# The drain of a two-layer attention kernel: last unit transposed on TensorE, a new order, a split form for four tiles

## The reference, cut to what matters

```python
h = _layernorm(x) * (1 + ca) + sa
x = x + ga * _L1_attn_ref(h, ...)       # latent attention, 32 heads, softmax over 512 keys
h = _layernorm(x) * (1 + cb) + sb
x = x + gb * _L1_ffn_ref(h, W, lora_A, lora_B, magnitude)

# _L1_attn_ref, per head:  attn = softmax(query @ key.T * scaling);  out = attn @ v;  return out @ w_o
# _L1_ffn_ref:
eff_W = W + lora_B @ lora_A
column_norm = sqrt(sum(eff_W * eff_W, axis=1))
result = (x @ W.T + x @ lora_A.T @ lora_B.T) / column_norm * magnitude
```

## Time and profile before

| | us |
|---|---|
| median of 3 runs (lowest, highest) | 905.48 (903.23, 910.38) |
| profiled execution, its own time | 904.65 |
| span of its profile | 902.4 |
| busy: TensorE, VectorE, GpSimd, ScalarE | 820.7, 681.8, 538.9, 536.5 |

### The profile page before, as it was taken

The page is one execution under the profiler, slowest core; times in us unless marked ns, Lnnn a source line. Parts: engine busy times, 40 slices in busy tenths (PEclk is TensorE's granted clock), DMA queues, the critical chain, the costliest instruction groups (busy, mean ns, idle before and its releaser), DMA issues.

```text
span 902.4 us, 15065 instructions
## 1 busy us (share of the span) xinstructions
PE 820.7 (91%) x4560; PEld 540.4 (60%) x4560; DVE 681.8 (76%) x1322; ACT 536.5 (59%) x1158; POOL 538.9 (60%) x481
## 2 busy tenths in 40 slices
PE   3899993699996996899999999999999999999997
PEld 1588873578784874465656565665655656564543
DVE  4768896644453467998989898889898899897662
ACT  5668874624233785666666666665666666665522
POOL 3334432012122236998889888887888989897213
PEclk8899997799998898999999999999999999999899
DMA  8530000845235441666666666665566766665511
GB/s 330 216 119 2 1 2 9 227 117 176 89 105 151 123 130 38 168 153 152 153 154 155 154 153 155 153 156 143 131 156 185 184 154 155 149 156 138 125 35 70
DMA packets 91460, 120.07 MB, mean 133 GB/s; under 512 B 30387, under 2 KB 41651, under 8 KB 91381
## 3 DMA queue, kind: packets, MB, share of 16 engines
q1 hardware_dynamic: 66804, 85.54, 34.3%
q10 hardware_dynamic: 24576, 33.59, 15.1%
HBM read 41.45 MB, written 2.10 MB: 48 GB/s over the span
## 4 chain that ended last, share of the span: by engine, by line
PE 45%; DVE 8%; issue 5%; ACTq 1%; ACT 1%; POOL 0%; DMA 0%; POOLq 0%; DVEq 0%; SPq 0%
PE bank L1536 11%; PE bank L1523 6%; PE bank L1524 4%; PE bank L1525 4%; PE bank L1550 4%; PE bank L1551 3%; PE bank L1552 3%; PE bank L1594 3%; DVE blk L1642 2%; DVE cT_lo L1714 2%; DVE stage_a L1178 2%; ACTq L1485 1%; DVE nmax L1626 1%; DVE stage_a L1181 1%; PE bank L1161 1%
## 5 line engine op out<-in xcount | busy, mean ns | idle before, releaser
L1626 DVE TENSOR_REDUCE nmax<-bank 128x1 f32<-128x512 f32 x256 | 174.1, 680 | 46.2 <-PE bank L1525 45.1
L1776 ACT ACTIVATE prob<-bank,nmax 128x512 f32<-128x512 f32 x172 | 118.3, 688 | 102.8 <-DVE nmax L1626 89.2
L1864 POOL TENSOR_TENSOR prob<-prob,rinv 128x512 f32<-128x512 f32 x129 | 132.6, 1043 | 33.4 <-DVE rinv L1634 32.0
L1523 PE MATMUL bank<-xk_hi,q_hi 128*128 128x512 f32 x256 | 113.2, 442 | 14.3 <-ACT prob L1776 8.5
L1642 DVE STREAM_TRANSPOSE blk<-prob 128x512 f32<-128x512 f32 x172 | 120.1, 698 | 6.3 <-ACT prob L1818 5.0
L1523 PEld LDWEIGHTS bank<-xk_hi,q_hi 128*128 128x128 f32 x256 | 48.5, 190 | 92.9 <-issue 53.0
L1524 PE MATMUL bank<-xk_lo,q_hi 128*128 128x512 f32 x256 | 102.0, 398 | 0.0
L1525 PE MATMUL bank<-xk_hi,q_lo 128*128 128x512 f32 x256 | 101.1, 395 | 0.0
L1195 POOL TENSOR_TENSOR q_lo<-stage_a,q_hi 128x512 fp32r<-128x512 f32 x64 | 82.2, 1285 | 25.1 <-ACT q_hi L1186 24.9
L1776 ACT ACTIVATE stage_a<-bank,nmax 128x512 f32<-128x512 f32 x84 | 57.8, 688 | 49.0 <-DVE nmax L1626 42.9
L1191 POOL TENSOR_TENSOR stage_a<-stage_a 128x512 f32<-128x512 f32 x64 | 82.9, 1295 | 4.8 <-DMA stage_a<-stage_a 4.8
(11 more groups left out here) (251 smaller groups left out, 1939.5 us busy)
## 6 DMA issues: line engine op xcount, KB each, us to landing
pT<-blk SPq DMA_DIRECT2D x256, 64.0 KB, 2.1
pT<-blk ACTq DMA_DIRECT2D x256, 64.0 KB, 2.1
raw_e<-blk SPq DMA_DIRECT2D x256, 64.0 KB, 2.1
raw_e<-blk ACTq DMA_DIRECT2D x256, 64.0 KB, 2.1
raw_e<-in_wo SPq DMA_DIRECT2D x16, 512.0 KB, 4.0
stage_a<-stage_a SPq DMA_DIRECT2D x128, 64.0 KB, 2.1
raw_e<-in_wmod SPq DMA_DIRECT2D x6, 1024.0 KB, 7.7
stage_a<-in_wmod SPq DMA_DIRECT2D x12, 512.0 KB, 4.4
```

Of the source, the lines that this page charges most:

```text
L1523: pe.matmul(sbk, q_hi[:, u % 2, q], xk_hi[:, 2, ks], start=True, stop=False)
L1626: dve.tensor_reduce(nmax[:, s % RING:s % RING + 1], s_bank[s % 2][:, :], AX.X, ALU.max, negate=True).then_inc(max_done, 1)
L1776: act.activation(prob[s % RING], s_bank[s % 2][:, :], ACT.Exp, bias=nmax[:, s % RING:s % RING + 1], accum_out=rsum[:, s % RING:s % RING + ...
L1864: pool.tensor_tensor(prob[s % RING], prob[s % RING], bc(rinv[:, s % RING:s % RING + 1], [P, S]), ALU.mult).then_inc(norm_pool, 1)
```

## The change

It touches only the last block, from round 248 on, and leaves the result the same.

- SP and ScalarE no longer move unit 63, and VectorE no longer turns it. Instead `last_T` transposes its four rounds on PE into two score banks and twice q_bank, and `last_turn` (VectorE) copies each into pT. ScalarE issues the first two moves of unit 62 before the last exponential and the other six behind the last normalization.
- After round 255 the loop ends, and each engine has a list. PE: last_T(0), last_T(1), both contexts of couple 30, last_T(2), last_T(3), sum_squares, both contexts of couple 31, tile_T(0), projections 30, tile_T(1), tile_y(0), projections 31, then tile_T(t+1), tile_y(t) for t = 1 to 7.
- The four squares are summed on VectorE (`add_squares`), so that `sum_squares` has one product. w_square comes one step earlier.
- Tiles 4 to 7 use the split form: w_eff and h are rounded by ScalarE (`w_round`, and behind `tile_h`), the rests taken by GpSimd (`w_rest`) and VectorE (`tile_lo`), and tile_y has 12 matmuls.
- ScalarE rounds tile 0's h ahead of couple 31's context. Tile 7's last addition is VectorE's.

```diff
 BA_AT = {247: 0, 249: 1, 251: 2, 253: 3}
-XT_AT = {259: 0, 263: 1, 267: 2, 271: 3}
-Y_AT = {263: (0,), 267: (1,), 271: (2, 3)}
...
+LAST = UNITS - 1
+tr_bank = (s_bank[0], q_bank, s_bank[1], q_bank)
+fw_hi = xk_lo[:, :, :].rearrange("p c s -> p (c s)").rearrange("p (k n) -> p k n", k=KC)
+fw_lo = xk_hi[:, :, :].rearrange("p c s -> p (c s)")[:, 0:KC * D].rearrange("p (k n) -> p k n", k=KC)
+fh_hi = q_hi[:, :, :].rearrange("p s (k n) -> p s k n", k=KC)
+fh_lo = q_lo[:, :, :].rearrange("p s (k n) -> p s k n", k=KC)
...
-STEPS = 8 * (COUPLES + 2) + 1
...
-        for u in range(UNITS):
+        for u in range(LAST):
...
-            sp.wait_ge(x4_done, t + 1)
+            if t + 1 < TILES:
+                sp.wait_ge(x4_done, t + 1)
+            else:
+                sp.wait_ge(x4_last, 1)
...
+                    if 2 * j + e < LAST:
+                        pT_ready(pe, 2 * j + e)
+                    else:
+                        pe.wait_ge(tr_done, TPB)
...
-            pe.wait_ge(wsq_done, KC)
-            pe.wait_ge(exp_done, ROUNDS - 1)
-            for k in range(KC):
-                mm = pe.matmul(n_bank[:, :], ones, w_sq[:, k, :], start=(k == 0), stop=(k == KC - 1))
-            mm.then_inc(norm_ps, 1)
+            pe.wait_ge(sq_done, KC - 1)
+            pe.wait_ge(tr_done, 1)
+            pe.matmul(n_bank[:, :], ones, w_sq[:, 0, :], start=True, stop=True).then_inc(norm_ps, 1)
+        def last_T(st):
+            s = LAST * TPB + st
+            norm_ready(pe, s)
+            if st == 0:
+                pe.wait_ge(exp_done, ROUNDS - 1)
+            elif st == 1:
+                pe.wait_ge(weff_done, KC)
+            elif st == 2:
+                pe.wait_ge(exp_done, ROUNDS)
+            else:
+                pe.wait_ge(tr_done, 2)
+            for kt in range(TPB):
+                mm = pe.transpose(tr_bank[st][:, kt * P:(kt + 1) * P], prob[s % RING][:, kt * P:(kt + 1) * P],
+                                  ident[:, :])
+            mm.then_inc(tr_ps, 1)
...
-                pe.wait_ge(weff_done, KC)
+                pe.wait_ge(tr_done, TPB)
...
+            if t < TPB:
+                pe.wait_ge(f_hf, t + 1)
+            else:
+                pe.wait_ge(f_lo, t - TPB + 1)
             if t == 0:
-                pe.wait_ge(exp_done, ROUNDS)
+                pe.wait_ge(tr_done, 3)
...
+            else:
+                if t == TPB:
+                    pe.wait_ge(fwlo_done, KC)
+                mm = split_matmuls(pe, y_bank[t % 2][:, :], [
+                    ((fh_hi[:, t % 2, c, :], fh_lo[:, t % 2, c, :]), (fw_hi[:, c, :], fw_lo[:, c, :]))
+                    for c in range(KC)])
...
+        last_T(0)
+        last_T(1)
+        context(COUPLES - 2, (0, 1))
+        context(COUPLES - 2, (2, 3))
+        last_T(2)
+        last_T(3)
+        sum_squares()
+        context(COUPLES - 1, (0, 1))
+        context(COUPLES - 1, (2, 3))
+        tile_T(0)
+        project_out(COUPLES - 2, (0, 1))
+        project_out(COUPLES - 2, (2, 3))
+        tile_T(1)
+        tile_y(0)
+        project_out(COUPLES - 1, (0, 1))
+        project_out(COUPLES - 1, (2, 3))
+        for t in range(1, TILES):
...
+        def last_turn(st):
+            dve.wait_ge(tr_ps, st + 1)
+            if st == 0:
+                dve.wait_ge(pv_ps, 2 * (COUPLES - 2))
+            dve.tensor_copy(pT[LAST % P_SLOTS].rearrange("p g (k t q) -> p t k g q", k=TPB, t=TPB)[:, st],
+                            tr_bank[st].rearrange("p (k g q) -> p k g q", k=TPB, g=QD)).then_inc(tr_done, 1)
+        def add_squares():
+            for k in range(1, KC):
+                dve.wait_ge(wsq_done, k + 1)
+                if k > 1:
+                    dve.wait_ge(sq_done, k - 1)
+                dve.tensor_tensor(w_sq[:, 0, :], w_sq[:, 0, :], w_sq[:, k, :], ALU.add).then_inc(sq_done, 1)
+        def context_rest(j):
+            dve.wait_ge(chi_done, j + 1)
+            dve.tensor_tensor(by_block(cT_lo[:, :]), ct_bank[:, :].rearrange("p (g t q) -> p g t q", g=QD, t=TPB),
+                              by_block(cT_hi[:, :].bitcast(F32)), ALU.subtract).then_inc(clo_done, 1)
+        def tile_lo(t):
+            dve.wait_ge(f_hi, t - TPB + 1)
+            dve.tensor_tensor(fh_lo[:, t % 2, :, :], f_h[:, t % 2, :, :], fh_hi[:, t % 2, :, :].bitcast(F32),
+                              ALU.subtract).then_inc(f_lo, 1)
...
+        last_turn(0)
+        row_inv(ROUNDS - 2)
+        last_turn(1)
+        add_squares()
+        last_turn(2)
+        last_turn(3)
+        context_rest(COUPLES - 2)
+        tile_rstd(0, TPB)
+        tile_xn(0)
+        tile_xn(1)
+        norm_inverse()
+        context_rest(COUPLES - 1)
+        factors()
+        tile_xn(2)
+        tile_gate(0)
+        tile_xn(3)
...
         gated(1, 0)
...
         tile_rstd(4, 6)
+        tile_gate(1)
         tile_xn(4)
-        tile_xn(5)
...
         tile_gate(2)
+        tile_xn(5)
         tile_rstd(6, 8)
+        tile_lo(4)
         tile_gate(3)
         for t in range(4, TILES):
+            if t + 1 < TILES:
+                tile_lo(t + 1)
             if t + 2 < TILES:
                 tile_xn(t + 2)
             tile_gate(t)
+        dve.wait_ge(yg_done, TILES)
+        dve.tensor_tensor(x[:, TILES - 1, :], x[:, TILES - 1, :], y_g[:, (TILES - 1) % 2, :],
+                          ALU.add).then_inc(x4_last, 1)
...
+            if t >= TPB:
+                act.wait_ge(f_hf, t + 1)
+                act.activation(fh_hi[:, t % 2, :, :], f_h[:, t % 2, :, :], ACT.Copy).then_inc(f_hi, 1)
+        def w_round(k):
+            act.wait_ge(weff_done, k + 1)
+            act.activation(fw_hi[:, k, :], w_eff[:, k, :], ACT.Copy).then_inc(fwhi_done, 1)
...
+            if s == ROUNDS - 1:
+                moves(LAST - 1, 0)
+            exps(s)
...
+            if s - 1 in BA_AT:
+                w_square(BA_AT[s - 1])
+        norm_row(ROUNDS - 1)
+        for jj in range(1, TPB):
+            moves(LAST - 1, jj)
+        context_round(COUPLES - 2)
+        tile_std(0, TPB)
+        out_weights(COUPLES - 2)
+        act.wait_ge(blo_done, WB_FREE)
+        column_norm()
+        act.wait_ge(s_ps, ROUNDS)
+        w_round(0)
+        w_round(1)
+        tile_h(0)
+        context_round(COUPLES - 1)
+        out_weights(COUPLES - 1)
+        tile_h(1)
+        w_round(2)
+        w_round(3)
+        tile_h(2)
+        tile_std(4, 6)
         tile_h(3)
-        tile_std(4, 6)
-        tile_h(4)
         tile_std(6, 8)
-        for t in range(5, TILES):
+        for t in range(TPB, TILES):
...
+        def w_rest(k):
+            pool.wait_ge(fwhi_done, k + 1)
+            pool.tensor_tensor(fw_lo[:, k, :], w_eff[:, k, :], fw_hi[:, k, :].bitcast(F32),
+                               ALU.subtract).then_inc(fwlo_done, 1)
...
+        normalize(ROUNDS - 2)
+        out_weights(COUPLES - 2)
+        w_rest(0)
+        w_rest(1)
+        out_weights(COUPLES - 1)
+        w_rest(2)
+        w_rest(3)
+        for t in range(TILES - 1):
```

More of the change, by code:

```diff
@@ L1592, in tile_y @@
                             pe.wait_ge(yg_done, t - 1)
-                        for c in range(KC):
-                            mm = pe.matmul(y_bank[t % 2][:, :], f_h[:, t % 2, c, :], w_eff[:, c, :],
-                                           start=(c == 0), stop=(c == KC - 1))
+                        if t < TPB:
+                            for c in range(KC):
+                                mm = pe.matmul(y_bank[t % 2][:, :], f_h[:, t % 2, c, :], w_eff[:, c, :],
+                                               start=(c == 0), stop=(c == KC - 1))
+                        else:
[4 more added lines that the diff above has]
+                                for c in range(KC)])
                         mm.then_inc(y_ps, 1)
-                    for s in range(STEPS):
-                        if s < ROUNDS:
-                            scores(s)
+                    for s in range(ROUNDS):
+                        scores(s)
                         if s % TPB == 0 and s // TPB + 2 < UNITS:
@@ L1701, in _ @@
                         rotate(dve, 1, part)
[L1702 to L1705, removed]
+                    for s in range(ROUNDS):
+                        row_max(s)
+                        if s % 2 == 0 and 2 <= s:
                             row_inv(s - 2)
-                        if TURN_LAG <= s < ROUNDS + TURN_LAG:
+                        if TURN_LAG <= s < LAST * TPB + TURN_LAG:
                             turn(s - TURN_LAG)
@@ L1710, in _ @@
                             rotate(dve, s // TPB + 2, ROPE_AT[s % TPB])
[L1711 to L1714, removed]
[L1715 removed]
+                        if s % 8 == 4 and 0 <= s // 8 - 2:
+                            context_rest(s // 8 - 2)
                         if s - 1 in BA_AT:
                             w_sum(BA_AT[s - 1])
[L1718 to L1729 removed]
                         n = s - 8 * (HP + 2)
@@ new lines, in moves, with context_round @@
+                    def moves(m, jj):
```

(25 more changed lines are left out.)

70 lines of the change are left out of this document (18 added, 52 removed).

## The result

Timed beside the kernel before on the same chip, the changed kernel took 901.32 us (median of 7 runs, 899.89 to 903.39) against 906.63 (7 runs, 903.23 to 910.38). The ratio is 0.9944, 95% interval 0.9919 to 0.9969: faster by half a per cent. I had forecast 900.7. The profiled execution has a span of 897.9 against 902.4; I had worked out 898.0.

A forecast was written before the change was run, and what follows sets the result against it. PE, almost without a break, was taken to bound the drain: 9.2 us off and 4.8 back gave -4.4, span 902.4 to 898.0. Forecast 900.7, between 900.25 (profiled execution) and 901.1 (median); range 896 to 905.5.

The forecast's parts named there:

- Contexts 31 early, behind one short wait: PE after the sum of squares: contexts 31 start near 853.9, after a new wait of 0.80 for cT_lo.
- The late landing of unit 62's moves: Before contexts 31: unit 62's last DMA move lands at 853.4, at slowest 854.1; landing of moves costs up to +0.2.
- The transposes buy nothing by themselves but the early contexts 31: Unit 63 on PE: its moves were not in the chain, so transposing only buys the right to early contexts 31.
- The sum of squares: PE before contexts 31: one product with ones instead of four takes 3 x 0.91 off PE; additions hide under contexts 30.
- my ledger: Account of PE's drain: 9.2 us off in all, 4.8 back, for a gain of 4.4.
- The split form gives 2.5 and takes 2.3 back: Tiles 4 to 7: shorter y saves 2.5 on PE, longer hand-offs between engines return 2.3.
- GpSimd's four rests of w_eff and ScalarE's roundings lie in idle time: Split form's preparation on GpSimd and ScalarE: costs nothing; rests (1.29 each) done by 867, wanted at 879.5.
- The unknown costs: Drain: last_turn, VectorE's addition, landing of moves, product with ones, hand-offs, slack before y(4); together some -1 to +3.
- rival C: VectorE in the drain: slow permuted write (+1.4) and longer hand-offs (+1.2) leave -1.8, giving 903.3; chance 14%.
- the old fall: PE clock after the wait ending at 838.23: half clock for 6.9 us, a loss of some 3.4, expected to stay.
- rival A: PE from 853.1: the wait drops the clock, later waits and transposes keep it down 17 us, giving 909; chance 6%.
- the waits of 1.34 and 1.67: PE before projections 31 and before T(5): both waits vanish, taking 1.34 and 1.67 off by the chain.

The follow-up runs named there:

- e8: Kernel before, with squares one step earlier, added on VectorE between the turns of rounds 253 and 254, and one product with ones: drain 58.38 against 55.62 us.
- e6: Kernel before, with the squares added on VectorE behind the turn of round 254 and one product with ones instead of four: drain 57.06 against 55.62 us.

## Why the prediction was right, point by point

Times from the start of the drain, as predicted (less 846.85) and as measured (less 846.08):

| | predicted | measured |
|---|---|---|
| contexts 31 | 7.05 | 7.19 |
| T(1) | 13.88 | 14.07 |
| T(2) | 20.57 | 21.25 |
| T(5) | 32.21 | 32.93 |
| y(4) | 32.65 | 34.17 |
| T(6) | 36.37 | 37.15 |
| T(7) | 40.53 | 41.25 |
| y(7) | 44.22 | 44.89 |
| end of the span | 51.15 | 51.82 |

The forecast's 846.85 is the chain's start, the measured 846.08 the list's. By the chain's start, 846.25, every measured row is 0.17 less: T(1) is then 0.02 late, T(2) 0.51 and the end 0.50.

- **Contexts 31 early, behind one short wait.** Right: 0.68 for cT_lo, where I had 0.80. The late landing of unit 62's moves did not show.
- **The transposes buy nothing by themselves but the early contexts 31.** Half shown: with the moves back contexts 31 start 3.8 later and the drain is 5.9 longer. That the transposes buy nothing in the old order was not tried.
- **The sum of squares.** Its 2.7 off PE stands in my ledger. No run puts the four products back into the new order; that it holds there is argued only from the trace, where PE waits no more than 0.68 behind the one product. Taken alone it is worth less than nothing, in three placements. The ledger's items are not each worth their entry; they are PE's list only as long as no other engine is later.
- **The split form gives 2.5 and takes 2.3 back.** Right for the last tiles, wrong for the whole. From T(5) to the last gate it saves 0.24, but T(2) comes 0.5 later with it, and in sum it costs 0.4. The waits before T(6) and T(7) are the ones I had worked out (T(5) to T(6) to T(7) 4.22 and 4.10, predicted 4.16).
- **The step that failed** is "GpSimd's four rests of w_eff and ScalarE's roundings lie in idle time". They lay in GpSimd's idle time, but VectorE paid: factors and xn(2) took 5.6 (861.71 to 867.28) instead of some 2.8. Of the 2.8 more, 1.0 is the multiplication beside couple 31's b_lo, which stays in the runs without the split form and with the rests early; the other 1.8 are the two rests, which go in both, and with them the lateness of T(2). So the term that the forecast put at nothing cost 0.5 at T(2) (20.74 without it, 21.25 with it), and that went through to the end: 51.65 by the chain against 51.15. It also made tile_std(6, 8) late, which stands ahead of h(4) on ScalarE, and so y(4) by 0.65. That cost little more, as T(6) waited for xn(6) in any case: 0.17, by the slowed lo(5).
- **The unknown costs.** last_turn, given 0.55 to 1.4, took 0.65 to 0.69; the addition on VectorE took 0.69, as put into the sum. So VectorE was late as in rival C, mildly, and by a cause that C did not name.
- **The clock.** I kept the old fall and counted no new one. No stretch behind 846 was below 1.00 in the changed kernel, with eight and eight transposes around contexts 30 and one wait of 0.68. By the rule cited from the Trainium skill (TensorE: Matmul & The Clock Gate, Part 4: PE-mode transpose) rival A would have been likelier; this trace gives it no support. The mechanism is real, though: in the runs with the moves back and in e8 longer or repeated waits did bring half clock. The half-clock stretch ahead of the drain, which I kept at 6.9, lasted 3.4.
- **The total.** 898.0 forecast and 897.9 measured is closer than the working was. By the chain the drain was 0.50 longer than I had it, and its start 0.60 earlier, so the match is luck. The start moved because the half-clock stretch ahead of it lasted 3.4 instead of 6.9, worth some 1.7, while the execution had come there some 1.0 later. The second profile of the unchanged kernel had a stretch of 3.4 too, so that need be no effect of the change.
- **What no run separates.** The new order of PE, ScalarE and VectorE as a whole, to which the ledger gives the waits of 1.34 and 1.67: both are gone from the trace, but only two of its orders were undone (the moves back, couple 31's rounding ahead).

## What to carry to other kernels

An order change should be priced engine by engine: what PE gets rid of counts only up to the next engine's arrival, and the DMA issues in an engine's queue belong to that count. When elementwise work goes to an idle GpSimd, look at what VectorE does beside it, and lay it under matrix evictions or a reciprocal, not under operations that read two tensors from SBUF, nor under one like xn. To read gains of a few tenths of a per cent, compare a stretch that repeats (here the drain, to 0.1) rather than whole times, which scattered by 7 to 10 here.

## What the runs showed of the hardware

VectorE and GpSimd hold each other up in some pairs of operations, one until the other is through. A multiplication of two SBUF tensors on VectorE beside a GpSimd subtraction ends 0.55 after the latter does (1.70 instead of 0.69, in three kernels alike); three such additions took 2.24 with GpSimd idle, 2.76 or 3.13 with one operation beside them, 3.62 with two. xn, which has one SBUF input, is held too (1.40 for 0.55; 1.61 in the second profile of the unchanged kernel; xn(0) and xn(1) together 1.97 beside a b_lo, 1.00 without). Where xn began 0.31 ahead of b_lo it took 0.55, and b_lo 1.36. The reciprocal in place (3.34 either way) is not held. Nor are VectorE's operations with one of their two inputs in PSUM: these two took 1.28 with GpSimd's addition beside them, and the next two of the kind 1.27 without.

```profile
868.25 1.28 DVE L1697 TENSOR_TENSOR bank<-bank,gate 128x512 f32<-128x512 f32 x2
```
```profile
867.96 1.51 POOL L2010 TENSOR_TENSOR x_res<-x_res,wb_all 128x512 f32<-128x512 f32 x1 [0.96 <-DVE wb_all L1775]
```

The Trainium skill says this (SBUF — State Buffer, Who interferes with whom, and SBUF: two separate sides): a VectorE instruction with two SBUF inputs, against a GpSimd one that reads SBUF, or in a two-port mode takes a port pair shared with GpSimd as an exclusive lock for the whole instruction. The traces agree for the multiplications, with the numbers above; whether xn ran in such a mode no view here shows. Had I weighed that page, the failed step would have been a term.

Half clock on PE came in the wait of 4.79, which followed one of 1.47 (860.2 to 867.0), after waits of 1.00, 0.71 and 1.57 one close behind another (857.7 to 861.1), and, ahead of the drain, after the wait of 1.94 in ten profiles of thirteen. It did not come after single waits of 0.68, 1.38, 1.69, 2.23 or 2.65, nor after 1.77 and 1.57 in e6. So the length of a wait alone does not tell.
